# A graph-network kernel on TensorE: other starting addresses for three pairs of operands, and the short zero matmuls moved out of the loop

## What is computed

```python
def _L0_gnn_ref(node_features, adj_matrix, W, b):
    num_neighbours = adj_matrix.sum(axis=-1, keepdims=True)
    h = jnp.einsum('bni,io->bno', node_features, W) + b
    h = jnp.einsum('bnm,bmo->bno', adj_matrix, h)
    return h / num_neighbours
...
    def _gcn_layer(x, adj, W, b):
        support = jnp.einsum('bnf,fh->bnh', x, W)
        return jnp.einsum('bnm,bmh->bnh', adj, support) + b
    x = jax.nn.relu(_gcn_layer(batch_graph, adj, W1, b1))
    x = jax.nn.relu(_gcn_layer(x, adj, W2, b2))
    out = _gcn_layer(x, adj, W3, b3)
...
x = _layernorm(x + _L0_gnn_ref(x, adj, L0_gnn_W, L0_gnn_b), axis=-1)
x = _layernorm(x + _L1_gnn_ref(x, adj, ...), axis=-1)
```

## The kernel before

| stage | stationary, moving | matmuls x columns |
|---|---|---|
| p5(old) | s2, adj | 24 x 512 |
| p2(new) | x1, adj | 24 x 512 |
| p6(old) | x3, W | 24 x 256 |
| p3(new) | W, g | 12 x 512 |
| p7(old) | adj, s3 | 48 x 256 |
| p0(nxt) | xT, W | 24 x 256 |
| p4(new) | x2, W | 24 x 256 |
| p1(nxt) | adj, h | 48 x 256 |

## Time and profile before

### The profile page before, as it was taken

How to read it: one execution, slowest core, us unless ns; L and a number is a source line. 1 busy time by engine, 2 the same in 40 slices (tenths; PEclk the granted TensorE clock), 3 DMA queues, 4 the chain that set the end, 5 groups by cost and what they waited for, 6 DMA issues and landing times.

```text
span 549.3 us, 10686 instructions
## 1 busy us (share of the span) xinstructions
PE 537.1 (98%) x3695; PEld 496.8 (90%) x3695; DVE 347.2 (63%) x1032; ACT 306.6 (56%) x757; POOL 209.9 (38%) x225
## 2 busy tenths in 40 slices
PE   6899999999999999999999999999999999999996
PEld 6778998989899898998989899898998989899896
DVE  3874674756657475674756657475674756657546
ACT  4455646566555656656566555656656566554532
POOL 1954409063270814509063270814509063271100
PEclk8999999999999999999999999999999999999999
DMA  8630070511607033070511507033070521500002
GB/s 251 229 153 1 1 269 1 197 74 47 222 0 265 2 101 166 0 267 0 186 81 50 217 0 264 4 109 158 0 267 0 180 89 51 218 2 39 1 1 78
DMA packets 15286, 58.23 MB, mean 106 GB/s; under 512 B 1952, under 2 KB 2720, under 8 KB 13472
## 3 DMA queue, kind: packets, MB, share of 16 engines
q1 hardware_dynamic: 14688, 56.24, 28.4%
q10 hardware_dynamic: 576, 1.70, 0.9%
HBM read 49.55 MB, written 8.39 MB: 105 GB/s over the span
## 4 chain that ended last, share of the span: by engine, by line
PE 93%; DVE 3%; DMA 1%; ACT 1%; issue 1%; POOL 0%; SPq 0%; DVEq 0%; POOLq 0%
PE bank_a L173 16%; PE bank_a L174 16%; PE bank_a L175 16%; PE bank_b L173 15%; PE bank_b L174 15%; PE bank_b L175 15%; DMA xT_raw<-in_xT 1%; POOL adj_lo L867 0%; DVE stats L737 0%; ACT std L558 0%; DVE h_lo L637 0%; DVE xT_lo L637 0%; ACT x_hi L537 0%; DVE moments L749 0%; DVE v L730 0%
## 5 line engine op out<-in xcount | busy, mean ns | idle before, releaser
L846 POOL TENSOR_TENSOR adj_lo<-adj_raw,adj_hi 128x512 fp32r<-128x512 f32 x56 | 70.8, 1295 | 269.0 <-ACT adj_hi L459 269.0
L637 DVE TENSOR_TENSOR x_lo<-bank_a,x_hi 128x512 fp32r<-128x512 f32 x64 | 44.3, 691 | 69.5 <-ACT bank_a L539 69.5
L173 PE MATMUL bank_b<-h_hi,adj_hi 128*128 128x256 f32 (+1 forms) x272 | 75.6, 278 | 2.2 <-DVE h_lo L637 1.9
L175 PE MATMUL bank_b<-h_hi,adj_lo 128*128 128x256 f32 (+1 forms) x272 | 75.4, 277 | 0.0
L174 PE MATMUL bank_b<-h_lo,adj_hi 128*128 128x256 f32 (+1 forms) x272 | 75.4, 277 | 0.0
L514 ACT ACTIVATE std<-moments,eps_col 128x1 f32<-128x1 f32 x64 | 18.9, 295 | 95.5 <-DVE moments L707 95.5
L175 PE MATMUL bank_b<-s_hi,adj_lo 128*128 128x256 f32 x232 | 64.1, 276 | 0.0
L173 PE MATMUL bank_b<-s_hi,adj_hi 128*128 128x256 f32 x232 | 64.0, 276 | 0.0
L174 PE MATMUL bank_b<-s_lo,adj_hi 128*128 128x256 f32 x232 | 64.0, 276 | 0.0
L537 ACT ACTIVATE x_hi<-bank_a,b_col 128x512 fp32r<-128x512 f32 x64 | 43.8, 684 | 23.2 <-PE bank_a L175 22.0
L173 PEld LDWEIGHTS bank_b<-h_hi,adj_hi 128*128 128x128 f32 x272 | 51.1, 188 | 2.6 <-DVE h_lo L637 2.1
(11 more groups left out here) (109 smaller groups left out, 1632.1 us busy)
## 6 DMA issues: line engine op xcount, KB each, us to landing
adj_raw<-in_adjT SPq DMA_DIRECT2D x28, 512.0 KB, 5.4
adj_rows<-in_adj SPq DMA_DIRECT2D x14, 1024.0 KB, 9.4
out_y<-y SPq DMA_DIRECT2D x15, 512.0 KB, 2.9
xT_raw<-in_xT SPq DMA_DIRECT2D x14, 512.0 KB, 6.5
x_raw<-in_x SPq DMA_DIRECT2D x14, 512.0 KB, 7.4
w_raw<-in_w SPq DMA_DIRECT2D x4, 256.0 KB, 6.3
adj_raw<-in_adjT ACTq DMA_DIRECT2D x2, 512.0 KB, 6.6
adj_rows<-in_adjT SPq DMA_DIRECT2D x2, 512.0 KB, 5.9
```

The lines of the kernel that those rows point to most:

```text
L173: pe.matmul(acc, st[0], mv[0], start=start, stop=False)
L175: return pe.matmul(acc, st[1], mv[0], start=False, stop=stop)
L637: return dve.tensor_tensor(lo, full, hi.bitcast(F32), ALU.subtract)
L846: pool.tensor_tensor(adj_lo[:, s, k, :], raw[:, k, :], adj_hi[:, s, k, :].bitcast(F32), ALU.subtract).then_inc(adj_split, 1)
```

## The change

Two things. The pairs w and xT, x2, x3 trade places among the `sb` calls, so that w begins at 64 modulo 128 and xT, x2 and x3 at 0. adj, x1, s2 stay at 0, and g, s3, h at 64. Both calls of `seam` in the step are gone (with those in the stages behind it), and one stands ahead of the loop, behind a wait for the first tile of s2, which the loop's first matmul waits for as well.

| stage | start of stationary, moving modulo 128, before | after |
|---|---|---|
| p5, p2 | 0, 0 | 0, 0 |
| p6, p0, p4 | 64, 0 | 0, 64 |
| p3 | 0, 64 | 64, 64 |
| p7, p1 | 0, 64 | 0, 64 |

```diff
-        w_hi, w_lo = pair("w", [P, 4, KF, F])
         adj_hi, adj_lo = pair("adj", [P, RING, T, N])
         x1_hi, x1_lo = pair("x1", [P, T, F])
         s2_hi, s2_lo = pair("s2", [P, T, F])
+        xT_hi, xT_lo = pair("xT", [P, T, F])
+        x2_hi, x2_lo = pair("x2", [P, KF, N])
+        x3_hi, x3_lo = pair("x3", [P, KF, N])
 
 
         inv_rows = sb("inv_rows", [P, T], F32)
         std1 = sb("std1", [P, T], F32)
 
-        xT_hi, xT_lo = pair("xT", [P, T, F])
+        w_hi, w_lo = pair("w", [P, 4, KF, F])
         g_hi, g_lo = pair("g", [P, KF, N])
-        x2_hi, x2_lo = pair("x2", [P, KF, N])
-        x3_hi, x3_lo = pair("x3", [P, KF, N])
         s3_hi, s3_lo = pair("s3", [P, T, F])
         h_hi, h_lo = pair("h", [P, T, H_ROW])
@@ p0
                         pe.wait_ge(reader, at(read, T, j + 1))
-                        if j == 0:
-                            seam(banks[0])
@@ p6
                     pe.wait_ge(reader, at(read, T, j + 1))
-                    if j == 0:
-                        seam(bank_b[0])
-
@@ ahead of the loop
             p1(second, range(3, T))
+            pe.wait_ge(s2_split, 1)
+            seam(bank_a[0])
             with pe.Fori(0, TURNS - 1) as turn:
```

## The result

The changed kernel takes 558.46 us (median, 558.12 to 558.60), the kernel before 551.28 in the same comparison: a ratio of 1.0131, 95% interval 1.0115 to 1.0147. Its profiled execution took 558.6 us with a span of 556.7. Against the profiled execution of before that is 7.45 us more.

A forecast was written before the change was run, and what follows sets the result against it. PE's matmul pace was taken as the bound. 14 steps x (0.15 + 0.02 - 0.02) = 2.1 us less, 0.12 + 0.1 more, so 1.9 less: 549.25, plus 0.12 for the median, 549.4 us; range 547.0 to 552.6.

The forecast's parts named there:

- The reading of the bound: Whole loop: a step lasts as long as PE needs for its 228 matmuls and two seams.
- no wait of PE in a step: Sign in the profile after: PE waits for nothing within a step, which would then be 0.15 us shorter.
- p6 took 2.83: p6 without its seam: 24 matmuls at the slow gap, 2.83 instead of 2.85 us, a gain of 0.02 a step.
- p3 2.76: p3 with its new pair 64, 64: between 2.72 and 2.79 us, taken as 2.77, a loss of 0.02 a step.
- behind the steps: Stages after the loop: p4(LAST) 0.11 less, p6_last and p7(old, tile 3) 0.16 more, together about +0.1 us.
- The seam ahead of the loop: Ahead of the loop: the one remaining seam costs 0.12 us, once; its wait for s2 costs nothing new.
- p7's entry from p3 has to stay at the usual gap as it does today: Passage p3 to p7: p7 stays at 0.1133 us a matmul; called the weakest step.
- the likeliest case: Whole kernel: the forecast itself, 549.4 us, with p7 usual and p6 slow; chance 47%.
- I let p0 and p4 go on at the pace they inherit: p0 and p4 behind p7: usual gap continues without a seam, p0 in 2.72 us, a gain of 0.15 a step.
- p7 turns slow: Rival, p3 to p7: 144 matmuls 0.0045 slower, p5's start 0.02 more; step 0.52 longer, 558.9 us; chance 16%.
- Offsets play no part: Rival: slow pace comes with change of stage; p0 slow, p4 and p1 inherit it, 555.4 us; chance 4%.
- The gain of 0.15 us a step: p0: its seam disappears with the reversal between p7 and p0, 24 matmuls take 2.72 us, 0.15 less a step.

The follow-up runs named there:

- w1_at_64: split_w with W1 alone moved to 64 modulo 128, so that p3 reads both operands at 64 and p6 keeps its seam; 557.78 us, ratio 1.0121.
- split_w_no_seam: split_w without the seam of p6; 558.54 us, ratio 1.0141.
- split_w: Kernel before with W in four tensors: only p0 and p4 get the new addresses, p6's seam kept, p0's gone; 549.27 us, ratio 0.9963.
- after_gap64: Changed kernel with 64 bytes more between the operand groups, so stationary and moving stand 128 apart in p6, p7, p0, p4, p1; 564.00 us, ratio 1.0235.
- layout_only: Changed kernel's new addresses with the seams of p0 and p6 where they were before; 561.99 us, ratio 1.0194.

## Why the prediction was wrong

**The reading of the bound was right.** PE's pace is the time: no trace of these kernels has a wait of PE within a step, and "no wait of PE in a step" held in the changed one.

**Three terms came out as worked out.** p6 took 2.83, as taken from p7(old, tile 2); p3 2.76, where I took 2.77; behind the steps 0.08 us were added, where I took 0.1. The seam ahead of the loop cost 0.16 in place of 0.12, since p5 behind it took longer to settle.

**The step that failed** is "p7's entry from p3 has to stay at the usual gap as it does today". p7 went to the slow gap instead, 5.65 us for 48 matmuls in place of 5.44. The step was called the weakest step and got the likeliest case all the same. The reason given for it, that the moving operand stays at 64 there, is refuted: w1_at_64 shows the passage from 64, 64 to 0, 64 slow behind a settled p3. With it fell "I let p0 and p4 go on at the pace they inherit": they did inherit, but the slow pace.

**The chances were set against the evidence.** The forecast had p6 slow and never asked what a slow p6 hands to p3 and p3 to p7, though behind the steps it did let a slow p7(old, tile 2) hand its pace to p6_last. split_w_no_seam shows that this alone makes p7 slow. Of a chain in which each stage inherits, I had costed one link at a time. p7(old, tile 2) in the earlier trace rows, slow behind two equal offsets, was the nearest row for p7 as it was for p6; I used it for one and argued it away for the other.

**The rival "p7 turns slow" is what happened**, and its size was right: 144 matmuls at 0.0045 more, 558.9 forecast, 558.46 measured. Of its terms, 0.02 at p5 didn't come (5.47 before and after), and a step is 0.49 longer in place of 0.52.

**"Offsets play no part" falls**, and with it the Trainium skill's rule (TensorE: Matmul & The Clock Gate, Step-by-step: what each phase is for) as a guide to this case: moving nothing but addresses took split_w from 549.27 to 557.78 us (w1_at_64) and the changed kernel from 558.46 to 564.00 (after_gap64). By the rule, as the prediction read it, neither pair would differ. The runs don't show what inside TensorE or SBUF the two reads share, so how the pace comes about stays open.

**The gain of 0.15 us a step was real**: split_w has it, 549.27 us against a forecast of 549.4 for the change. The change moved W for p0 and p4, where that helps, and by the same stroke for p3, where it harms. It also dropped p6's seam, which ends the slow pace at p6's old distance, and gave p6 the distance at which layout_only's seam doesn't help.

## What to carry to other kernels

Where TensorE is the bound, read its pace from the starts of instructions, stage by stage, and look for the same stage at two paces: it shows that a pace is inherited, and then a change at one passage has to be costed through all stages behind it, to the next one that resets. Count the address distance between stationary and moving operand modulo 256 and with its sign. In this kernel 64 either way was the only distance with the usual pace at 256 columns, and the best layout was the one that kept it the same from p3 to p1, behind a p6 whose seam works. Test a new distance by moving a single tensor.

## What was not expected of the hardware

At 256 fp32 columns a matmul takes 0.120 us if its two operands' starts differ by 0 or 128 bytes modulo 256, and 0.113 or 0.118 at 64 either way, by how the stage was entered. Moving both by 64 changes nothing (549.36 us); moving one group by 128 does (551.64 against 549.27, 550.43 against 559.65), by 256 not (549.37). p1 holds both distances modulo 512 in each of these kernels (a row of h is 1280 bytes, not a multiple of 512) and keeps one pace. A short matmul of zeros ended the slow pace where the stationary operand stood 64 above the moving one, and never where it stood 64 below (six kernels). Where it worked, the zeros always stood 64 below the moving operand; where it failed, they stood 128 from it, 64 above or 64 below. So the zeros' own address doesn't save a stage at 64 below, but at 64 above no other address of theirs was tried. A pace can also turn without a change of distance: p7(LAST) of the kernel before follows a usual p7 at the same distance, begins with a gap of 0.18 us (538.67 to 538.85) and then runs at 0.118 to its end (544.26). At 512 columns equal offsets settle to 0.227 within some twelve matmuls; with the operands 64 apart p3 was at 0.229 behind a usual p6 and at 0.2335 behind a slow one, and p2 with its stationary operand 64 above at 0.2333. Why a reversal ends a slow pace and begins one behind a usual stage, why the sign matters, and why a seam helps on one side only, is described here and not explained.
